# A fused four-layer graph network: one-deep products made full depth, warming products placed in TensorE's waits, zeroing dropped, and edges weighted ahead of an adjacency

## The reference, cut to what matters

```python
# L0 gnn: graph attention, 8 heads, then a second attention layer with one head
h = (x @ W).reshape(n, H, C)
e = leaky_relu(alpha_s[src] + alpha_d[dst], 0.2)      # softmax per target over its edges
out = segment_sum(h[src] * alpha[:, :, None], dst)
# L0 ffn: top-2 of 8 experts (768->48->768) plus a scan "bk_green_diag" along the nodes
# L1 gnn: GCNConv(x) = D^-1/2 (A + I) D^-1/2 (x W) + b
# L1 ffn: two-level top-2 routing over 4 groups of 8 experts
# L2 gnn: relu(adj @ (x Wd Wu) W1 + b1), then adj @ (.) W2 + b2, adj built from edge_weight
# L2 ffn: ternary weights, 8-bit activations, width 32, gated
# L3 gnn: two GCNConv layers with a relu between
# L3 ffn: router MLP, 12-head attention, low-rank MLP
x = x + layer(norm(x))                                 # around every layer
```

## Time and profile before

| what | value |
|---|---|
| runs before, us | 377.79, 374.84, 377.69 (median 377.69) |
| profiled execution, us | 374.69 |
| its span, us | 372.9 |
| mean granted TensorE clock, share of full speed | 0.973 |
| TensorE matmul busy | 355.2 us (95%), 1612 records |
| VectorE busy | 180.4 us (48%) |
| ScalarE busy | 66.6 us (18%) |
| GpSimd busy | 39.3 us (11%) |
| HBM read | 89.53 MB, 241 GB/s over the span |

### The profile page before, as it was taken

How to read it: one execution, slowest core, us unless ns; L and a number is a source line. 1 busy time by engine, 2 the same in 40 slices (tenths; PEclk the granted TensorE clock), 3 DMA queues, 4 the chain that set the end, 5 groups by cost and what they waited for, 6 DMA issues and landing times.

```text
span 372.9 us, 4235 instructions
## 1 busy us (share of the span) xinstructions
PE 355.2 (95%) x1612; PEld 227.2 (61%) x1617; DVE 180.4 (48%) x547; ACT 66.6 (18%) x154; POOL 39.3 (11%) x61
## 2 busy tenths in 40 slices
PE   7999999899999999998999999987889999999997
PEld 3566665566565755555456556554446599967654
DVE  3936425584838375567636645407521501063341
ACT  2002110111011100112012211132113411064010
POOL 4910000010000002040040000121030100000000
PEclk9999999999999999988999999997969999999999
DMA  8999999988855949999985375776250700000001
GB/s 276 396 414 413 431 410 427 377 342 286 343 217 182 406 164 426 398 411 393 401 313 226 114 295 181 287 267 229 75 227 2 275 22 3 0 2 0 0 2 42
DMA packets 10502, 90.19 MB, mean 242 GB/s; under 512 B 2169, under 2 KB 2822, under 8 KB 6386
## 3 DMA queue, kind: packets, MB, share of 16 engines
q1 hardware_dynamic: 8238, 84.91, 57.7%
q0 software_dynamic: 848, 3.61, 2.8%
q10 hardware_dynamic: 1396, 1.40, 1.1%
HBM read 89.53 MB, written 0.39 MB: 241 GB/s over the span
## 4 chain that ended last, share of the span: by engine, by line
PE 84%; DMA 6%; DVE 6%; ACT 1%; issue 1%; SPq 1%; POOL 1%; DVEq 0%; POOLq 0%; ACTq 0%
PE ps L1491 15%; PE ps L1457 13%; PE ps L1841 8%; PE ps L1436 6%; DMA ring<-in_l_wu 6%; PE ps L1659 4%; PE ps L1678 4%; PE ps L1479 3%; PE ps L1368 3%; PE ps L1520 2%; PE ps L1917 2%; PE ps L1889 2%; PE ps L1937 2%; PE ps L1558 2%; PE ps L1758 2%; PE ps L1498 1%
## 5 line engine op out<-in xcount | busy, mean ns | idle before, releaser
L1457 PE MATMUL ps<-ring,xT 128*128 128x512 f32 (+1 forms) x168 | 56.4, 486 | 0.0
L1491 PE MATMUL ps<-ring,h 128*128 128x512 f32 (+1 forms) x168 | 55.6, 486 | 0.0
L1491 PEld LDWEIGHTS ps<-ring,h 128*128 128x128 f32 x168 | 31.2, 190 | 21.9 <-issue 20.1
L1457 PEld LDWEIGHTS ps<-ring,xT 128*128 128x128 f32 x168 | 30.8, 191 | 19.5 <-issue 17.7
L782 DVE CUSTOM_DVE_ANT_0 g<-h,avec 128x768 f32<-128x768 f32 x8 | 7.7, 959 | 36.7 <-ACT h L495 24.8
L495 ACT ACTIVATE h<-ps 128x768 f32<-128x768 f32 (+6 forms) x24 | 13.6, 577 | 61.7 <-PE ps L1457 16.2
L1436 PE MATMUL ps<-ring,xT 128*128 128x512 f32 (+1 forms) x72 | 24.1, 488 | 0.0
L870 DVE TENSOR_SCALAR ring<-ring,idxb,ewb 128x128 bf16<-128x128 bf16 x99 | 22.5, 310 | 0.0
L381 POOL TENSOR_TENSOR rstd<-var,mhalf 128x1 f32<-128x1 f32 x8 | 4.6, 579 | 147.0 <-DVE var L724 70.4
L1436 PEld LDWEIGHTS ps<-ring,xT 128*128 128x128 f32 x72 | 13.4, 190 | 9.0 <-issue 8.1
L1368 PE MATMUL ps<-shiftm 128*128 128x512 bf16 x41 | 14.5, 496 | 3.9 <-POOL shiftm L387 2.1
(11 more groups left out here) (395 smaller groups left out, 512.5 us busy)
## 6 DMA issues: line engine op xcount, KB each, us to landing
ring<-in_gat_w SPq DMA_DIRECT2D x15, 2304.0 KB, 11.4
avec<-in_gat_a SPq DMA_DIRECT2D x9, 768.0 KB, 8.8
ring<-in_l_w SPq DMA_DIRECT2D x3, 2304.0 KB, 15.7
ring<-in_gat_w SPq DMA_DIRECT2D x6, 384.0 KB, 6.1
ring<-in_l_w SPq DMA_DIRECT2D x2, 1152.0 KB, 12.7
ring<-in_l1f_w1a SPq DMA_DIRECT2D x1, 2304.0 KB, 13.0
ring<-in_l1f_w1b SPq DMA_DIRECT2D x1, 2304.0 KB, 10.3
ring<-in_l1f_w2a SPq DMA_DIRECT2D x1, 2304.0 KB, 11.8
```

Of the source, the lines that this page charges most:

```text
L1457: last = mm(ps[:, at + lo:at + hi], xT[:, c, :], w[:, c, lo:hi], start=(c == 0), stop=(c == C - 1))
L1491: last = mm(ps[:, 4 * WIN + lo:4 * WIN + hi], h2[:, par * D + c * P:par * D + (c + 1) * P], w[:, c, lo:hi], start=False, stop=False)
```

## The change

On SyncE the load of head 1's W1 is issued ahead of the first `avec`. The zeroing of the two banks goes, with `zrow`; the first of the products that add into a bank starts it instead. The count and head 0's score row move into head 1's product, after three chunks. On VectorE the first 20 edges are weighted ahead of `whole_adjacency(0)`. In the first expert block two chunks of the hidden product move into the gate product, warming products are added behind the green levels, and the turn of `comb` is put ahead of that of `l2_wu`. The tail's product takes 128 rows instead of 11 (zeros in the others, by two memsets on GpSimd), and two bias products take the identity and 128 rows instead of a row of ones and one row. Warming products are added at eight further places.

```diff
@@ SyncE
+            load_w1(1, 1)
             load_avec(0)
-            load_w1(1, 1)
@@ GpSimd
-            pool.memset(zrow[:], 0.0).then_inc(s("constants"), 1)
...
+            pool.memset(combT[:], 0.0).then_inc(s("bk_const"), 1)
...
+            link(pool.memset(g3[:], 0.0))
             pool.tensor_tensor(g3[0:11, :], g2[0:11, :], g1[0:11, :], ALU.mult).then_inc(s("tail_ready"), 1)
@@ VectorE
-            whole_adjacency(0, adj1T)
             dve.wait_ge(s("ew_parts"), 1)
             weigh_edges(0)
+            whole_adjacency(0, adj1T)
@@ TensorE, heads
-                                  w[:, c, lo:hi], start=False, stop=False)
+                                  w[:, c, lo:hi], start=(n == 0 and c == 0), stop=False)
...
-            pe.wait_ge(s("constants"), 5)
-            for lo, hi in HALVES:
-                mm(ps[:, 4 * WIN + lo:4 * WIN + hi], zrow[:], zrow[:, 0:1].broadcast_to([1, hi - lo]), start=True, stop=False)
...
-            head_product(1, 1, 16, lambda: turn_attention(0)).then_inc(S["hprod"], 1)
+            head_product(1, 1, 16, lambda: turn_attention(0), count_edges).then_inc(S["hprod"], 1)
@@ TensorE, first expert block
-            warm_until(9, "var_ready", 2)
+            warm_until(11, "var_ready", 2)
...
             for c in range(C):
                 wait_T(2, c)
                 last = mm(bank(7, E0 + 1), xT[:, c, :], gatew[:, c * (E0 + 1):(c + 1) * (E0 + 1)],
                           start=(c == 0), stop=(c == C - 1))
+                if c in (1, 3):
+                    hidden_first(c // 2)
...
+            hidden_first(2)
+            shift_green(0)
+            for c in range(3, C):
+                last = hidden_first(c)
+            last.then_inc(s("hid0_mm"), 1)
+            for lv, n in ((1, 4), (2, 4), (3, 4)):
+                shift_green(lv)
+                stay_warm(n, 1)
...
             shift_green(4)
-            stay_warm(1, 1)
+            stay_warm(2, 1)
...
+            pe.wait_ge(s("comb_ready"), 1)
+            tr(bank(7, P, 0, 11), comb[:, 0:11], ident).then_inc(s("combT_ps"), 1)
             wait_unit(pe, U_L2)
...
-                mm(ps[:, 2 * WIN + lo:2 * WIN + hi], combT[0:11, :], g3[0:11, lo:hi], start=False, stop=True) \
+                mm(ps[:, 2 * WIN + lo:2 * WIN + hi], combT[:], g3[:, lo:hi], start=False, stop=True) \
@@ TensorE, second GCN block
+            mm(bank(1, HID2), ident, row("l2_b1"), start=True, stop=False)
             pe.wait_ge(s("l2_copied"), 3)
             mm(bank(0, HID2), zT[0:DOWN + 1, :], up_first, start=False, stop=True).then_inc(s("l2_ps"), 1)
-            mm(bank(1, HID2), ones[0:1, :], row("l2_b1")[0:1, :], start=True, stop=False)
+            stay_warm(2, 4)
             pe.wait_ge(s("node_rows"), 1)
             mm(bank(1, HID2), adj2T[:], g2[:, 0:HID2], start=False, stop=True).then_inc(s("l2_ps"), 1)
+            stay_warm(2, 4)
             pe.wait_ge(s("node_rows"), 2)
...
             last.then_inc(s("l2_ps"), 1)
+            stay_warm(2, 4)
             pe.wait_ge(s("l2_copied"), 4)
@@ TensorE, last graph layer and bit layer
+            warm_until(6, "var_ready", 6)
+            stay_warm(2)
             transpose_rows(xn, "early_copied", {0: 3, 3: 4})
...
             early(1, range(1, C)).then_inc(s("early_ps"), 1)
+            stay_warm(2)
             pe.wait_ge(s("bits_ready"), 3)
...
             pe.wait_ge(s("in_l3_b1"), 16)
+            stay_warm(2)
             for n in range(2):
                 pe.wait_ge(s("early_copied"), 6 + n)
-                mm(even(2, n), ones[0:1, :], avec[0:1, n * EVEN:(n + 1) * EVEN], start=True, stop=False)
+                mm(even(2, n), ident, avec[:, n * EVEN:(n + 1) * EVEN], start=True, stop=False)
```

More of the change, by code:

```diff
@@ L143, in build @@
         ones = sb("ones", [P, P])
-        zrow = sb("zrow", [1, P])
         gatew = sb("gatew", [P, C * (E0 + 1)])
@@ L152, in build @@
         identb = sb("identb", [P, P], BF16)
-        combT = sb("combT", [32, P])
+        combT = sb("combT", [P, P])
         cells = sb("cells", [P, 128])
@@ L615, in _ @@
             act.wait_ge(s("l2_ps"), 3)
-            act.wait_ge(s("constants"), 6)
+            act.wait_ge(s("constants"), 5)
             nc.scalar.activation(zT[0:DOWN, :], bank(7, P, 0, DOWN), ACT.Relu, bias=bias1[0:DOWN, 0:1]) \
@@ L1016, in _ @@
             link(nc.vector.tensor_scalar(level, level, -2.0, None, ALU.add))
-            dve.wait_ge(s("bk_const"), 9)
+            dve.wait_ge(s("bk_const"), 10)
             nc.vector.tensor_copy(directions[:, :, 0:6:5], level.unsqueeze(2).broadcast_to([P, 2, 2])) \
                 .then_inc(s("green_state"), 1)
-            dve.wait_ge(s("constants"), 7)
+            dve.wait_ge(s("constants"), 6)
             pick_first(1, lin[:, 0:E0], 1, E0)
@@ L1116, in _ @@
             dve.wait_ge(s("combT_ps"), 2)
-            nc.vector.tensor_copy(combT[:], bank(7, P, 0, 32)).then_inc(s("combT_ready"), 1)
+            nc.vector.tensor_copy(combT[0:32, :], bank(7, P, 0, 32)).then_inc(s("combT_ready"), 1)
             hidden_bias(1)
@@ L1521, in _, with count_edges @@
             last.then_inc(S["hprod"], 1)
-            pe.wait_ge(s("constants"), 5)
-            for lo, hi in HALVES:
-                mm(ps[:, 4 * WIN + lo:4 * WIN + hi], zrow[:], zrow[:, 0:1].broadcast_to([1, hi - lo]), start=True, stop=False)
[L1527 to L1531, removed]
-            head_product(1, 1, 16, lambda: turn_attention(0)).then_inc(S["hprod"], 1)
+            def count_edges():
+                pe.wait_ge(s("onehots"), 2)
+                for e in range(EC):
+                    last_ = mm(bank(3, P), oh_dst[:, e, :], oh_src[:, 0, e, :], start=(e == 0), stop=(e == EC - 1))
+                last_.then_inc(s("counted"), 1)
+                score_row(0, 0)
+            head_product(1, 1, 16, lambda: turn_attention(0), count_edges).then_inc(S["hprod"], 1)
             aggregate_head(0, 0)
@@ L1571, in _, with hidden_first @@
             wait(pe, "attnT_ready", 9)
-            warm_until(9, "var_ready", 2)
+            warm_until(11, "var_ready", 2)
             stay_warm(1)
             transpose_rows(xn, "xn_ready", in_halves(2))
+            wait_unit(pe, U_L0)
+            w = unit(U_L0, "l0_w1", "p (c n) -> p c n", c=C)
+            def hidden_first(c):
+                return mm(bank(0, H0), xT[:, c, :], w[:, c, :], start=(c == 0), stop=(c == C - 1))
             for c in range(C):
@@ L1619, in _ @@
             last.then_inc(s("l2_ps"), 1)
-            pe.wait_ge(s("comb_ready"), 1)
-            tr(bank(7, P, 0, 11), comb[:, 0:11], ident).then_inc(s("combT_ps"), 1)
             pe.wait_ge(s("combT_ready"), 1)
@@ L1694, in _ @@
             for lo, hi in HALVES:
-                mm(ps[:, lo:hi], combT[:], g1[0:32, lo:hi], start=True, stop=False)
+                mm(ps[:, lo:hi], combT[0:32, :], g1[0:32, lo:hi], start=True, stop=False)
             hidden_out(0)
```

## The result

The changed kernel took 365.86 us in the median of five executions (365.45 to 368.48), the kernel before 377.69 beside it (374.77 to 377.92): a ratio of 0.9724, with a 95% interval of 0.9668 to 0.9781. The forecast was 366.5. The ratio is that of the means; the quotient of the two medians is 0.9687, since three of five executions of before and one of five of after took some 3 us longer than the others of their kernel.

The account below looks back on a forecast made before the run. TensorE was taken as the bound (84% of the span), with four stretches at half clock. Gains of 2.1 + 0.25 + 1.3 + 1.3 + 3.3 = 8.2 us took the profiled 374.7 to 366.5, range 364.3 to 371.5.

Parts of the forecast that it names:

- Start: Start of the kernel: zeroing dropped, head 1's weights and product earlier; 0.4 us of 1.3 stays (bounds 0 and 1.3).
- Fourth head: Fourth head: edges before adjacency remove TensorE's wait of 1.73; 2.1 us gained up to here, start included (bounds 1.5 and 2.9).
- First expert block: First experts, 157 to 184: gate delay and saved waits even, swapped turns gain 0.25 us (bounds: loss 1.0, gain 1.1).
- Second GCN block: 246 to 254: bias product loses 0.43, four records at full clock gain; net 1.3 us (bounds: loss 0.43, gain 1.7).
- Graph and bit layer: 254 to 268: warming products fill TensorE's idle time, eight records run at full clock; gain 1.3 us (bounds 0 and 1.5).
- End of that block: 270 to 278: bias records and warming products at 2.4 instead of 1.2 GHz; gain 3.3 us (bounds 0 and 3.3).
- Depth costs nothing by itself: TensorE products: one-deep records take no less time than full-depth ones, so the gain must come from elsewhere.
- The 3.0 between profile and median of before: Whole kernel: profile 3.0 us under the median, taken for one more half-clock stretch the fillers would close; median kept at 366.5.
- falls without a gap stay: Rival, 13%: clock falls not preceded by long idling remain, only the third is mended; 372.6 us.
- HAM oscillation: Rule against the change: falls come from long idle gaps, so fillers in short waits mend nothing, only the third fall.
- One stretch that moves: Rival, 23%: one half-clock stretch stays or moves, giving back 1.3, 1.7 or 3.3 us; 368 to 370.
- The slower rival: Rival, 3%: half clock through 165 to 180, sets of four warming products outlast their levels; 379.4 or 382.4 us.

Follow-up runs that it names:

- avec_first: Changed kernel with the first row of attention vectors loaded ahead of head 1's W1 again; 367.39 us.
- count_first: Changed kernel with the count and head 0's score row ahead of head 1's product again, without the zeroing; 366.68 us.
- edges_back: Changed kernel with the adjacency scaled ahead of the fourth head's first 20 weighted edges again; 367.54 us.
- gate_apart: Changed kernel with the gate product in one piece again and the two hidden chunks behind it; 366.07 us.
- no_fill: Changed kernel without the warming products that the change added, full-depth products and new order kept; 373.12 us.
- no_fill_c: Changed kernel without the eight warming products ahead of the last graph layer's transposes, all others kept; 367.27 us.
- no_fill_d: Changed kernel without the two pairs of warming products in the bit layer, bias products at full depth; 365.89 us.
- shallow: Changed kernel with the tail product at 11 rows and both bias products one row deep again, warming products kept; 367.31 us.

## Why the prediction was right

The forecast and its sign were right, 366.5 against 365.86, and so was the mechanism of the large terms: the falls closed in all four places, and the wait at the fourth head went. Its sum was 8.2; the profile shows 8.8. The two smallest terms came out near their numbers for other reasons than those given, and one step, on the median of before, failed. By its own steps:

- **Start, 0.4 (bounds 0 and 1.3).** It gained 0.73. TensorE's part held roughly: head 1's weights at 16.43 against a predicted 16.4, the turn at 24.35 against 24.0, so 0.7 to 0.8 was gained there and not 1.3. The loss behind it did not come. I had let the next row of `avec` hold VectorE back and leave 0.4; it landed at 27.3, and VectorE waited for the copy of head 1's product, which moved with TensorE, by 0.73 (28.15 against 28.88). That the term was near is in part luck: the gain at the turn was put too high and then cut for a reason that did not hold. avec_first and count_first show that both moves were needed, as the step had it.
- **Fourth head, 1.7.** 1.94 between the first and the fourth head. The wait of 1.73 is the whole of what the order does (edges_back gives 1.66 back), and 0.2 more comes from the turn behind it, which takes 0.33 after a wait and 0.11 without one. Start and fourth head came to 2.67 against 2.1; this is the largest miss of the sum, inside its bounds of 1.5 and 2.9.
- **First expert block, 0.25.** 0.45. The two sides of the exchange that I took as even are not: the interleaved gate costs 0.9 (gate_apart), and the warming products give back 1.5 (from the block's transposes to `comb` 21.08 in no_fill, 19.62 with them). Against before, that chain got 0.8 shorter (19.62 against 20.41), and then waits 0.42 for the DMA that I had named as the limit. That load landed 2.5 earlier than before, a little less than the 2.67 of lead. All of the term is the swap of the two turns: from the landing to the tail it is 0.55 (180.59 to 181.14) instead of 1.13 (183.13 to 184.26), 0.58 where I had counted 0.25, since the turn of `comb` and VectorE's copy are done before `l2_wu` is there.
- **Second GCN block, 1.3.** 1.20: the bias product costs 0.43 in the chain, as forecast, and 0.07 came back ahead of it; the four records took 2.00 instead of 3.56, so 1.56 came back.
- **Graph and bit layer, 1.3.** 1.32. no_fill_c gives 1.4 for the eight products alone, and shows the whole course: idle 2.58, half clock, eight records in 4.16.
- **End of that block, 3.3.** 3.10 (3.18 with the 0.08 at the bias). The pair of 0.43 under the wait of 0.67, as costed at nothing, is indeed worth nothing and costs nothing (no_fill_d). For the largest term I had named no filler of its own but that pair, and it is not what holds the clock: without it the clock doesn't fall, without all the fillers it does, and without the eight ahead of the transposes it doesn't fall there either (no_fill_c, 1.89 for the eight products). Something ahead of it keeps the end of the block at 2.4 GHz; which products do is not shown.
- **Depth costs nothing by itself.** Borne out in length: the four one-deep bias records took 1.55 and the full-depth ones 1.56. Whether depth does anything for the clock is open, as said above.
- **The 3.0 between profile and median of before.** This step failed. I took it for one more stretch at half clock that the fillers would close. Of seven executions of before beside the last experiments, three with a granted clock of 0.973 took 377.1 to 377.7 and another with the same 0.973 took 374.98; and the changed kernel too had one of five at 368.48, with a clock of 0.995, above four at 365.45 to 365.88. A clock of 0.995 is also what shallow and no_fill_c have, each with one fall and 1.4 us more, so a fall may be about half of the 2.6 there; that execution has no profile to show it. So the higher times aren't a matter of stretches at half clock alone, and they are still there after. The forecast for the median came out by luck in this respect: most executions of after happened to be quick ones. The ratio looks 0.4% better than the two profiles do (365.88 to 374.69 is 0.9765), for the same reason. None of the longer executions was profiled, so what they are stays open.

The rivals: that falls without a gap stay was wrong as the changed kernel shows, and right for no_fill in one respect, since it ended 0.5 above the 372.6 worked out for it. That sum has a slip, 1.3 for two hidden chunks at half clock, where four records of 384 columns come to 2.6 by the rates of the earlier trace rows; the gate product did not fall in no_fill, so it was not put to the test. The Trainium skill, "TensorE: Matmul & The Clock Gate", section "HAM oscillation", which I set against the change, is nearest to the fall in no_fill_c, behind one idle stretch of 2.58; but the waits it tells of are for DMA, and this one is for ScalarE. The same page's section "A second HAM failure mode: psum-queue depth-cycling" tells of a kernel whose clock swings because TensorE is often idle for a short while between groups of matmuls, as it cycles through PSUM banks. The falls of no_fill behind waits of 0.5 to 1.3 are nearer to that, with 0.52 as the longest wait in the 3 us before the one at 248, though the waits here are for VectorE and ScalarE. One stretch that moves was seen in shallow (1.8), at the place of the fourth fall, so that chance was not empty. The slower rival, sets of four at 1.2 GHz, did not come: at 2.4 GHz they took 1.02 each. But one of them ends 0.03 before the next level's shift starts (169.51 + 1.02 against 170.56), so four is the most that fits there; sets of three were not tried.

## What to carry to other kernels

Read the granted clock by stage before costing anything: here TensorE, 95% busy, hid four stretches at 1.2 GHz, and dummy products in waits that were already lost bought some 7 of 8.8 us, while the reordered work bought 2.7 up to the fourth head and, without the products, lost 1.1 of it in the two blocks behind. A filler pays if it ends before the wait does, and it is worth trying to take each out again, since the two pairs in front of the largest fall were worth nothing. When two things arrive together at a block's end (a routing chain and a load within 1 us), price what each would give alone: 0.9 us saved on one of them was swallowed until the other was moved too.

## What was not expected of the hardware

- A fall of the clock is not fixed by the instructions around it. The same four one-deep records followed by the same eight warming products ran at 2.4 GHz in one kernel (1.90 for the eight) and at 1.2 in another (3.42), with TensorE without a recorded wait in the 4 us ahead of either but one of 0.40.
- The granted clock in the rows reads 1.00 at the very start, where the twelve warming products take 0.44 each (5.30), twice the 0.24 that they take later. Here the start's half clock has to be read from durations. Those twelve took between 4.05 and 5.30 from kernel to kernel, and it did not matter, since head 1 waits for its weights: with the twelve done in 4.56, the wait for W1 is 0.71, and head 1 starts at 16.41.
- Issuing 768 KB behind a 2304 KB load instead of ahead of it let that load land 1.8 us earlier (16.4 in the changed kernel, 18.2 in avec_first and before), the 1.8 that the prediction had. But only 1.3 of it is time in the queue (12.3 against 13.6 after its issue), less than the 1.8 worked out from the two landings in the earlier trace rows; the rest is that it is issued earlier itself (4.09 against 4.67). Between kernels with the same order it landed 12.0 to 12.7 after its issue.
